# Attention in a macaron block: the values with 64 columns of ones become the weight tile, the probabilities move

## The reference

```python
q = (x @ Wq + bq).reshape(Bv, Tv, 16, 8)
k = (x @ Wk + bk).reshape(Bv, Tv, 16, 64)
v = (x @ Wv + bv).reshape(Bv, Tv, 16, 64)
qc = jnp.einsum('bthd,dl->bthl', q, Wc)
att = jnp.einsum('bthl,bshl->bhts', qc, k) * SCALE
att = jnp.where(causal[None, None], att, -jnp.inf)
att = jax.nn.softmax(att, axis=-1)
y = jnp.einsum('bhts,bshl->bthl', att, v).reshape(Bv, Tv, 16 * 64)
return y @ Wo + bo
```

## Time and profile before

| what | value |
|---|---|
| median of the runs | 1134.17 us |
| span of the profiled execution, from first to last instruction | 1172.3 us |
| PE busy in the span | 972.9 us, 5887 matmuls |
| DVE busy | 548.8 us |
| ACT busy | 356.1 us |
| POOL busy | 365.8 us |
| DMA, moved | 76.31 MB, 65 GB/s mean |
| mean granted TensorE clock | 0.945 |

### The profile page before, as it was taken

One profiled execution on the slowest core, in us unless ns is written; L12 is line 12 of the kernel. 1 busy time (PEld: TensorE's weight loads), 2 busy tenths in 40 slices (PEclk: granted clock), 3 DMA queues, 4 the chain that ended last, 5 costly groups with the idle time before them and its releaser, 6 DMA issues.

```text
span 1172.3 us, 17171 instructions
## 1 busy us (share of the span) xinstructions
PE 972.9 (83%) x5887; PEld 752.4 (64%) x5887; DVE 548.8 (47%) x1503; ACT 356.1 (30%) x701; POOL 365.8 (31%) x550
## 2 busy tenths in 40 slices
PE   2305699999198999999999999999999653999994
PEld 1203366666134888979888498887999632666663
DVE  7533244444536674727273556362712541444444
ACT  2100122222023335343432443434353210222222
POOL 2736435555100311111110011444421073355551
PEclk9998899999579999999999999999999775999997
DMA  9400234453400000000000000101000002344435
GB/s 362 166 24 27 58 93 142 146 164 99 147 18 0 19 1 19 1 19 1 19 1 1 0 20 1 37 20 38 19 1 1 28 27 58 105 142 147 153 96 183
DMA packets 79285, 76.31 MB, mean 65 GB/s; under 512 B 10409, under 2 KB 69947, under 8 KB 78454
## 3 DMA queue, kind: packets, MB, share of 16 engines
q1 hardware_dynamic: 70006, 63.15, 17.3%
q0 software_dynamic: 9216, 12.33, 3.1%
HBM read 48.13 MB, written 30.21 MB: 67 GB/s over the span
## 4 chain that ended last, share of the span: by engine, by line
PE 72%; DVE 10%; issue 7%; another core or an unknown queue 6%; DMA 2%; ACT 2%; SPq 1%; POOL 1%; DVEq 0%; POOLq 0%; ACTq 0%
PE PS L1232 22%; PE PS L1143 8%; PE PS L1212 7%; PE PS L1129 6%; PE PS L1194 6%; PE PS L1130 5%; PE PS L1174 3%; PE PS L1283 3%; PE PS L1151 2%; PE PS L1197 1%; PE PS L1176 1%; PE PS L1109 1%; PE PS L1267 1%; DVE xs L899 1%
## 5 line engine op out<-in xcount | busy, mean ns | idle before, releaser
L1232 PE MATMUL PS<-area_v,pT 128*128 128x128 f32 x2304 | 316.5, 277 | 2.9 <-POOL pT L463 2.9
L1232 PEld LDWEIGHTS PS<-area_v,pT 128*128 128x128 f32 x2304 | 305.3, 192 | 13.3 <-POOL pT L463 3.0
L605 ACT ACTIVATE pT<-PS 128x512 f32<-128x512 f32 (+3 forms) x384 | 185.1, 490 | 250.6 <-PE PS L1212 244.8
L463 POOL TENSOR_SCALAR_AFFINE_SELECT pT<-pT 128x128 f32<-128x128 f32 x256 | 78.7, 311 | 469.4 <-ACT pT L605 468.3
L917 DVE TENSOR_REDUCE mxp<-PS 128x2 f32<-128x1024 f32 (+2 forms) x192 | 180.6, 955 | 83.0 <-PE PS L1197 62.2
L482 POOL DMA_INDIRECT ybuf<-area_o,yidx x160 | 155.4, 971 | 184.1 <-DVE area_o L876 143.3
L451 POOL DMA_INDIRECT xbuf<-xn,sidx x128 | 124.6, 974 | 130.6 <-DVE sidx L812 67.0
L1212 PE MATMUL PS<-Qc,Kz 128*128 128x512 f32 (+3 forms) x384 | 156.4, 411 | 7.8 <-ACT pT L605 5.3
L1143 PE MATMUL PS<-area_v,area_o 128*128 128x128 f32 (+1 forms) x768 | 126.5, 291 | 0.0
L1194 PE MATMUL PS<-Kz,Qn 128*128 128x512 f32 (+3 forms) x384 | 117.9, 389 | 4.1 <-DVE mxp L917 3.3
L1143 PEld LDWEIGHTS PS<-area_v,area_o 128*128 128x128 f32 (+1 forms) x768 | 93.9, 172 | 31.8 <-issue 11.3
(11 more groups left out here) (172 smaller groups left out, 945.1 us busy)
## 6 DMA issues: line engine op xcount, KB each, us to landing
area_v<-xbuf SPq DMA_DIRECT2D x32, 340.0 KB
area_v<-in_L_ffn_wg_dram SPq DMA_DIRECT2D x32, 256.0 KB
area_v<-in_L_ffn_wu_dram SPq DMA_DIRECT2D x32, 256.0 KB
area_v<-in_L_ffn_wd_dram SPq DMA_DIRECT2D x64, 128.0 KB
yg<-ybuf SPq DMA_DIRECT2D x24, 256.0 KB, 4.4
xbuf<-Kz SPq DMA_DIRECT2D x4, 1360.0 KB, 10.3
ybuf<-Kz SPq DMA_DIRECT2D x2, 2048.0 KB
Kz<-Kn SPq DMA_DIRECT2D x32, 128.0 KB
```

What stands on the lines that cost most here:

```text
L463: nc.gpsimd.affine_select(out=block_, in_=block_, pattern=[[1, P]], compare_op=ALU.is_ge, fill=zero, base=0, channel_multiplier=-1).then_i ...
L605: nc.scalar.activation(pT[:, N % 4, 0:w], PS[:, 4 + N % 2, 0:w], ACT.Exp).then_inc(exp_done, 1)
L1232: ins = mm(PS[:, 6 + half, (i % 4) * P:(i % 4 + 1) * P], pT[:, N % 4, k * P:(k + 1) * P], area_v[:, (j * NH + h) * VW:(j * NH + h) * VW + ...
```

## The change

The value product is turned round. The weight tile is now 64 latents of values beside 64 columns of ones, and the probabilities move, 256 tokens at a time, two heads in one step. The product leaves latents on partitions and 64 equal copies of the sums on the other 64 partitions. For the two heads of a pair the halves are mirrored. ACT copies the sums across to the partitions of the latents (`denominators`), DVE takes the reciprocal of a whole 128 x 256 tile and multiplies each half. The result is already the transposed tile that the output projection wants, so the transposes and copies of `out_rows` go.

With it come: 40 steps a group instead of 48; scores for the exponentials in pieces of at most 256 tokens for two heads; row maxima in 40 pieces of at most 256 keys for two heads, each pair in one bank, spread over steps 7 to 36; one causal mask matmul for two heads; queries and keys made one after the other in the same two banks, with the key product waiting for DVE's split of the queries; the causal masks on POOL twice a step; four banks for the output of the value product; and the ones, written once by POOL. Small tiles share memory with others.

```diff
-VW = LAT + 1
+VP = 3 * LAT
...
+TC = 256
+NCH = T // TC
+STEPS = [(c, j, p) for c in range(NCH) for j in range(2 * c + 1, -1, -1) for p in range(2)]
+SLOT = len(STEPS)
 LAG = 3
...
+DIAG = [n for n, (c, j, p) in enumerate(STEPS) if j >= 2 * c]
+UNIT_END = [[max(n for n, (c, j, q) in enumerate(STEPS) if (c, q) == (u, p)) for p in range(2)] for u in range(NCH)]
+ROWS = [(i, c, min(TC, (i + 1) * P - c * TC), hp) for i in range(HT) for c in range(1 + i // 2) for hp in range(2)]
+NS = len(ROWS)
+AT_Q, AT_QSPLIT, AT_K, AT_KSPLIT, AT_COMB, AT_TR, AT_CNT, AT_SLOTS, AT_S0 = 0, 1, 3, 4, 2, 5, 5, 6, 7
+AT_ROWS = [AT_S0 + k * 30 // NS for k in range(NS)]
+AT_MAX, AT_MT, AT_QC = AT_S0 + 30, AT_S0 + 30, AT_S0 + 31
...
@@ stream of ACT
+                    for u in range(NCH):
+                        for p in range(2):
+                            if n == UNIT_END[u][p] + LAG + 1:
+                                denominators(Gi, u, p)
...
+            def denominators(Gi, u, p):
+                X = 2 * (NCH * Gi + u) + p
+                bank = pv_bank(Gi, u, p)
+                act.wait_ge(pv_done, SLOT * Gi + UNIT_END[u][p] + 1)
+                if X >= 2:
+                    act.wait_ge(norm_done, X - 1)
+                nc.scalar.activation(den[0:LAT, p], PS[LAT:P, bank, 0:TC], ACT.Copy)
+                nc.scalar.activation(den[LAT:P, p], PS[0:LAT, bank, TC:2 * TC], ACT.Copy).then_inc(den_ready, 1)
...
@@ stream of DVE
-                link(nc.vector.reciprocal(rec[:, half], o[:, :, LAT:VW]))
...
+            def normalise(Gi, u, p):
+                X = 2 * (NCH * Gi + u) + p
+                dve.wait_ge(den_ready, X + 1)
+                link(nc.vector.reciprocal(den[:, p], den[:, p]))
+                bank = pv_bank(Gi, u, p)
+                out_ = yT[:, 2 * (Gi % NG) + p, u * TC:(u + 1) * TC]
+                tt(out_[0:LAT], PS[0:LAT, bank, 0:TC], den[0:LAT, p], ALU.mult)
+                tt(out_[LAT:P], PS[LAT:P, bank, TC:2 * TC], den[LAT:P, p], ALU.mult).then_inc(norm_done, 1)
...
             def heads(Gi):
...
+                            if n == UNIT_END[u][p] + LAG + 2:
+                                normalise(Gi, u, p)
...
@@ stream of PE
-            def qk(Gi):
+            def qk(Gi, q):
...
+                if q:
+                    pe.wait_ge(qk_split, 2 * Gi + 1)
...
+                for c in range(2):
+                    mm(PS[:, c, :], w[:].rearrange("p h r -> p (h r)")[:, gc], xnT[:, b * T + 512 * c:b * T + 512 * c + 512],
+                       start=True, stop=False)
...
             def s_rows(Gi, s):
...
+                    ins = mm(PS[:, s % 2, hh * w:(hh + 1) * w], Qx[Gi % 2][:, i * P:(i + 1) * P],
+                             Kz[Gi % 2][:, 2 * hp + hh, TC * c:TC * c + w], start=(hh == 0), stop=not diag, skip_group_check=True)
+                if diag:
+                    ins = mm(PS[:, s % 2, 0:2 * w].rearrange("p (h w) -> p h w", h=2)[:, :, w - P:w], identb[:],
+                             causS[:].unsqueeze(1).broadcast_to([P, 2, P]), start=False, stop=True, skip_group_check=True)
...
             def s_cols(Gi, n):
...
+                for a in range(2):
+                    ins = mm(PS[:, 2 + N % 2, a * w:(a + 1) * w], Kz[Gi % 2][:, 2 * p + a, j * P:(j + 1) * P],
+                             Qx[Gi % 2][:, t1 - w:t1], start=(a == 0), stop=True, skip_group_check=True)
...
             def pv(Gi, n):
...
-                    ins = mm(PS[:, 6 + half, (i % 4) * P:(i % 4 + 1) * P], pT[:, N % 4, k * P:(k + 1) * P],
-                             area_v[:, (j * NH + h) * VW:(j * NH + h) * VW + P],
-                             start=(first and k == 0), stop=(i == j), skip_group_check=True)
+                for a in range(2):
+                    h = (Gi % NG) * HG + 2 * p + a
+                    ins = mm(PS[:, pv_bank(Gi, c, p), (a + 1) * TC - w:(a + 1) * TC], value_and_ones(j, h), pT[:, N % 4, a * w:(a + 1) * w],
+                             start=(first and a == 0), stop=(j == 0), skip_group_check=True)
...
             def out_rows(b):
-                pe.wait_ge(norm_done, 2 * NH * (b + 1))
+                pe.wait_ge(norm_done, 2 * NCH * NG * (b + 1))
...
-                    for c in range(8):
-                        ins = nc.tensor.transpose(flat(2 * (i % 2), 2)[:, c * P:(c + 1) * P], os_[:, i, c * P:(c + 1) * P], ident)
-                    ins.then_inc(yt_ps, 1)
...
+                    out_proj(b, i)
```

More of the change, by code:

```diff
@@ L200, in program @@
         pT = sb("pT", [P, 4, 512])
-        rec = sb("rec", [P, 2, 4, 1])
+        bqf, bkf = [pT[0:2, k, :].rearrange("p (h r) -> p h r", r=RW) for k in range(2)]
+        wq_in = pT[:, 2, 0:P].rearrange("p (h d) -> p h d", d=HD)
+        bq2 = pT[0:2, 2, P:2 * P].rearrange("p (h d) -> p h d", d=HD)
+        bor = pT[0:1, 2, 2 * P:3 * P]
+        cen, cenn = [pT[0:G + E, 3, k * P:(k + 1) * P] for k in range(2)]
+        bqs = Qx[0][0:2, 0:NH * RW].bitcast(F32)
+        den = sb("den", [P, 2, TC])
         area_o = sb("area_o", [P, HT * NH * LAT])
-        area_v = sb("area_v", [P, HT * NH * VW + P - VW])
+        area_v = sb("area_v", [P, HT * NH // 2 * VP])
         def parts(area, first, *shapes):
@@ L1018, in _ @@
                 if b == 0:
-                    qk_parts(0)
+                    for q in range(2):
+                        qk_part(0, q)
                     for s in range(NS):
@@ L1243, in heads @@
                     if Gi + 1 < B * NG:
-                        if n == AT_QK:
-                            qk(Gi + 1)
-                        if AT_S0 <= n < AT_MAX:
-                            s_rows(Gi + 1, n - AT_S0)
+                        if n == AT_Q:
+                            qk(Gi + 1, 0)
+                        if n == AT_K:
+                            qk(Gi + 1, 1)
+                        for s in range(NS):
+                            if n == AT_ROWS[s]:
+                                s_rows(Gi + 1, s)
                         if n == AT_MT:
@@ L1320, in _ @@
                 if b == 0:
-                    qk(0)
+                    for q in range(2):
+                        qk(0, q)
                 for j in range(2 if b == 0 else HT):
```

239 lines of the change are left out of this document (94 added, 145 removed).

## The result

The changed kernel takes 1290.78 us (median, 1285.44 to 1292.11); the kernel before took 1134.41 beside it. The ratio is 1.137, with a 95% interval of 1.135 to 1.140. The sign was forecast, the size was not: +156 us instead of +99, and outside the range, which ended at 1272. Of all the runs behind this document one is left out of its ratio: it ran at a mean granted clock of 0.82 and took 1306.50 us, where the same kernel otherwise took 1228.49 to 1239.60.

The account below looks back on a forecast made before the run. TensorE's own work was taken to set a group. Group waits, the stage before group 0, output savings and clock summed to +99 us on the 1134.2 median, giving 1233; forecast 1205 to 1255 (0.60), range 1155 to 1272.

Parts of the forecast that it names:

- the clock: TensorE drops to half clock after a hole, costing 1.6 us each; in half of seven groups, +6 us, ends 0 and +22.
- the 3.4 us hole ahead of the row scores: TensorE idles 3.4 us at step 7 of a regular group, waiting for the DMAs that spread K.
- The base of the sum: A regular group's TensorE work is 58.4 us before and 58.8 after; the other 2.4 today are waits near its start.
- The part forecasts: TensorE work per group after: value product 31.2 us, scores for exponentials 9.2, row scores 11.7, query and key products 5.8.
- The reciprocal: On VectorE a 128x256 reciprocal takes 1.8 us, bounds 0.42 and 2.1, making one normalisation 2.7 us instead of 0.6.
- (a): Rival: the reciprocal is cheap, a normalisation 1.3 us, a group +4.6, total 1165 us (1150 to 1185); chance 0.14.
- The waits of a regular group: TensorE waits sum to 14.3 us, making a group 73.1 us instead of 61, about +12.2; four such groups +49.
- Group 1's layer norm: The layer norm on VectorE stands ahead of Q's split in group 1: +17.5 us for the group.
- group 4's routing: 9.6 us of routing on VectorE, part ahead of Q's split, part between K's split and the first maximum: +17 us.
- The transposes: Output stages lose eight transposes a tile, 0.96 us, 7.7 a stage, but start later: net -3.1 each, -6.2 together.
- (c): Rival, worse: reciprocal takes 2.1 us and the clock drops twice in each group: 1262 us, 1255 to 1290; chance 0.14.
- (b): Rival, faster: VectorE's bursts and K's spread vanish under TensorE's work, a group +0.2, total 1122 to 1128 us; chance 0.09.

Follow-up runs that it names:

- the filled holes' price: Changed kernel with idle 512-wide products where TensorE waits, in groups and ahead of output stages: 1267.55 us, ratio 1.117.
- the first and the fifth experiment: Both on the changed kernel: first, reciprocal of only 4 columns, 1202.02 us; fifth, logarithm and exponential on ScalarE instead of the reciprocal, 1200.13 us.
- the late row scores: Changed kernel with logarithm and exponential on ScalarE and row scores started at step 10 instead of 7: 1182.88 us, ratio 1.039.
- ten single holes: Kernel before with TensorE waiting empty-handed for two scratch reciprocals on VectorE at steps 12 and 46 of groups 1, 2, 3, 5, 6: 1230.10 us, ratio 1.051.
- two kernels that differ only ahead of the output stages: Changed kernel with logarithm and exponential and row scores from step 10, 1182.88 us; the same with five idle products ahead of each output stage, repeated, 1184.37 us.
- the kernel before with filled holes: Kernel before with the same ten waits, four idle 512-wide products issued ahead of each: 1210.16 us, ratio 1.032.

## Why the prediction was wrong

**The step that failed is the clock.** The prediction took one drop of 3.2 us in half of seven groups, 6 us in all, with 22 as the far end, and priced it by one short row. The trace has drops of 3.4 to 13.7 us, one to four of them in a group, and 172 us more at half clock than before. The short row was a lone hole in a kernel otherwise busy; the changed group 2 has six holes of over 1.2 us. The forecast also hung the drop on the 3.4 us hole ahead of the row scores. In groups 3, 5 and 6 that hole never opened, and the 27 us each at half clock came behind holes of 0.82, 2.22 and 2.34 us, all of them in the forecast's own walk. By the filled holes' price (a quarter of a us in groups, 0.44 in output stages) the extra 147 us in groups cost 37 and the 24 in output stages 10.6: 47 us where 6 were counted. That is 41 of the 57 us missed. The sum is worked out from these prices; what the fillers took back in a run is 23 us, with 80 of the 191 us at half clock left.

Two prices stand side by side, 0.41 and 0.25, because a slow TensorE also waits less. Group 2 is 60.6 us of work, 13.6 idle, and 3.8 left for 10 us of half clock. Group 6 is 60.6, 9.9 idle (by the same reading) and 11.4 left for 27. Both are about 0.4 a us, and 3.7 us of it comes back as shorter waits.

**The base of the sum.** "The other 2.4 us of a group today are waits near its start" was wrong. Without idle time before's group has 60.0 us from start to start and 0.5 of waits, so 1.9 of the 2.4 is work, which the changed kernel keeps. It then has 60.6 (forecast 58.8). The part forecasts missed in both directions: row scores 15.0 for 11.7, the value product 27.2 for 31.2, scores for the exponentials 11.8 for 9.2, and the two products with the queries and keys 5.8 as forecast. The record's price was right: 16 value records of 256 take 3.62 us, the last of them 0.38, so 0.216 each. Since starts overlap, the last record ahead of another line takes less, and a line's share is loose; the sum is not. About 1.3 to 1.8 us a group, some 10 to 12 in all, and it is most of what the clock leaves of the miss. Two us in the stage before group 0 and two in group 7 I did not follow up.

**Right, with their sizes:**
- The reciprocal: 1.753 us, forecast 1.8, from rows of 4 and 8 elements. The slope of the same operation was the right guide. The table of the Trainium skill, "VectorE: DVE Perf Modes", section "The TRN2 errata — SBUF-src ops pay a fixed extra latency per instruction", which would have made rival (a), does not hold for a reciprocal: 1753 ns measured for an estimate of 0.33 us. The repeat count of 8 in the same page's section "First, the fixed hardware budget", as an estimate 2.3 us, is nearer but above the row.
- The waits of a regular group at full clock, group 2: 13.6 of 14.3. Q's split 1.28 for 1.4, K's DMA 3.06 for 3.4, the bursts 4.0 and 3.9 for 3.6 each, the transposes of the maxima 0.57 for 0.5. The two row maxima behind the normalisation of step 8 (0.7) left no wait.
- Group 1's layer norm and group 4's routing ahead of Q's split: with a quarter of a us for each us at half clock taken off, +18.5 and +17.9 for +17.5 and +17. Group 0: +11.7 for +10.5.
- The transposes: a tile takes 2.39 us at full clock against 3.27, so 0.88 for the 0.96 counted, 7.0 a stage. The stage starts 5.35 us late, 5.4 forecast. It is longer than before for one reason, the clock after that start:

```profile
682.49 0.79 PE L1296 MATMUL PS<-brow,cst 1*128 1x128 f32 x2 [5.35 <-DVE area_o L973]
...
686.92 0.79 PE L1296 MATMUL PS<-brow,cst 1*128 1x128 f32 x2
...
694.07 0.48 PE L1296 MATMUL PS<-brow,cst 1*128 1x128 f32 x2
...
696.47 0.48 PE L1296 MATMUL PS<-brow,cst 1*128 1x128 f32 x2
```

The first tiles are 4.4 us apart, the later ones 2.4. The forecast gave no clock to the one stage whose hole it had itself found the longest.

**The rivals.** (c) had the mechanism of the clock, twice a group, but priced at the short row; its lower half closed the range, and the result lies 0.8 us above its upper end, 1290. Its other half, a reciprocal of 2.1 us, did not come, so that it lies so near is luck: a dearer reciprocal was counted where a dearer clock was. (a), the cheap reciprocal, is what the first and the fifth experiment build: 1200 instead of the 1165 forecast for it, and with the late row scores 1183. (b), faster, was to decide at the point where K lands before step 7. With K's wait cut away and the reciprocal gone the kernel is still 4% slower: the value product turned round saves about 2 us a group and the row scores and their masks take 2.8 back, so the most there was to gain is the output's 7 us a stage.

## What to carry to other kernels

When a change cuts holes into a TensorE that was busy throughout, price the clock with all holes in view, the short ones too, and not the longest alone: here ten single holes of 3.6 us cost 2.0 us each on top, the holes of group 2 another 3.8, and those of group 6 another 11.4, of which 3.7 came back as shorter waits. Before a number per token is written out in 64 copies for layout's sake, price what is done with it per element: 128x4 became 128x256, and 64 reciprocals cost 89 us. An engine with half its time free is free only between the moments when others wait for it.

## What the runs showed of the hardware

- A reciprocal on VectorE takes 1753 ns for 256 elements a partition, and 178 for 4: 6.25 ns an element, where a multiply of 256 takes 0.42 us.
- The granted clock falls to 0.50 after holes of the same length in one execution and not in another: after 0.82 us in group 6 of two kernels that differ only ahead of the output stages, once for 10 us and once not; after 3.63 us nine times of ten, for 3.4 or 6.8 us. In the changed kernel the longest drops of a group, 13.7 us, start at the 0.82 us hole and not at a longer one.
- A us at half clock costs 0.41 us where TensorE sets the pace (empty against filled holes), 0.46 in the projection (tiles of 4.4 and 2.4 us), and about 0.25 net in the changed kernel's groups, where waits for VectorE shrink by it (27 against 10 us at half clock in groups 5 and 6).
- Idle products in a hole kept the clock: the kernel before with filled holes has no half clock in the groups that have them, where empty ones brought 44 us. They pay only where they fit: +0.6 to +1.3 us a group where the clock did not change.
- ScalarE writes from one half of the partitions to the other at its usual price: 381 ns for 64x256, 383 for the 128x256 exponential of the earlier trace rows.
